# The two writes of the gate rows to DRAM, issued by ScalarE instead of SyncE

## The reference

```
x = x + attention(channel_norm(x))         # 8x8 windows, 4 heads of 16 channels, a bias per head and offset
t = tokens(x)                              # 65536 tokens of 64 channels
p = softmax(norm(t) @ router_w + router_b) # 8 experts
top_p, top_i = top_k(p, 2);  top_p = top_p / sum(top_p)
t = t + sum over the two chosen experts of  top_p * (norm(t) @ expert_w[i] + expert_b[i])
```

## Time and profile before

| what | value |
|---|---|
| median of 3 runs | 1083.46 us |
| the profiled execution | 1089.38 us |
| its span | 1087.6 us |
| PE busy | 1017.8 us, 94% |
| DVE busy | 826.2 us, 76% |
| ACT busy | 797.9 us, 73% |
| POOL busy | 431.8 us, 40% |
| mean granted TensorE clock | 0.988 |

### The profile page before, as it was taken

The page is one execution under the profiler, slowest core; times in us unless marked ns, Lnnn a source line. Parts: engine busy times, 40 slices in busy tenths (PEclk is TensorE's granted clock), DMA queues, the critical chain, the costliest instruction groups (busy, mean ns, idle before and its releaser), DMA issues.

```text
span 1087.6 us, 39027 instructions
## 1 busy us (share of the span) xinstructions
PE 1017.8 (94%) x16762; PEld 577.2 (53%) x16762; DVE 826.2 (76%) x1355; ACT 797.9 (73%) x1280; POOL 431.8 (40%) x509
## 2 busy tenths in 40 slices
PE   4898899999999999999999999999999999999868
PEld 3455555555555545556556555555565555555322
DVE  4456887877787778777877787787887887788873
ACT  1498888778788778878888787877888887677410
POOL 1002434334444443444434433444344335544440
PEclk9999999999999999999999999999999999999988
DMA  6003777877777678777777887777777886766764
GB/s 200 1 16 84 160 160 180 205 184 163 179 183 182 169 188 200 173 176 184 170 183 172 199 204 182 172 177 176 175 184 184 205 196 163 174 146 148 194 157 117
DMA packets 44199, 181.20 MB, mean 167 GB/s; under 512 B 9918, under 2 KB 10174, under 8 KB 27900
## 3 DMA queue, kind: packets, MB, share of 16 engines
q1 hardware_dynamic: 44028, 178.71, 68.8%
HBM read 151.15 MB, written 18.87 MB: 156 GB/s over the span
## 4 chain that ended last, share of the span: by engine, by line
PE 84%; DVE 6%; ACT 5%; issue 3%; DMA 1%; POOL 1%; SPq 0%; DVEq 0%; ACTq 0%
PE bank L713 20%; PE bank L592 12%; PE bank L609 11%; PE bank L626 7%; PE bank L566 5%; PE bank L536 5%; PE bank L633 5%; PE bank L576 4%; PE bank L645 3%; PE bank L654 2%; PE bank L664 2%; PE bank L513 2%; ACT lg L1281 2%; DVE gz L1872 2%; PE bank L527 1%
## 5 line engine op out<-in xcount | busy, mean ns | idle before, releaser
L713 PE MATMUL bank<-gz,wex 64*64 64x512 f32 x2048 | 253.4, 606 | 3.5 <-DVE ob L1921 3.5
L1850 DVE TENSOR_REDUCE mx<-bank 128x16 f32<-128x1024 f32 x128 | 156.2, 1220 | 109.0 <-PE bank L592 108.6
L1659 POOL TENSOR_TENSOR gz<-gz,tt 128x1024 f32<-128x1024 f32 x94 | 226.8, 2427 | 25.6 <-DMA gz<-gates_dram 25.6
L1872 DVE TENSOR_TENSOR gz<-gz,tt 128x1024 f32<-128x1024 f32 x156 | 200.9, 1306 | 1.6 <-DMA gz<-gates_dram 1.5
L1857 DVE TENSOR_TENSOR probs<-bank,mx 128x1024 f32<-128x1024 f32 x128 | 156.7, 1224 | 43.7 <-PE bank L609 40.6
L1620 POOL TENSOR_TENSOR tt<-prj,xs 128x512 f32<-128x512 f32 x64 | 81.7, 1300 | 251.9 <-ACT prj L1270 251.9
L609 PE MATMUL bank<-cst,probs 128*128 128x128 f32 x1024 | 166.6, 285 | 1.8 <-ACT pt L1253 1.3
L1253 ACT ACTIVATE pt<-bank 128x512 f32<-128x512 f32 x256 | 151.0, 590 | 21.9 <-PE bank L609 19.7
L609 PEld LDWEIGHTS bank<-cst,probs 128*128 128x128 f32 x1024 | 108.1, 140 | 97.7 <-issue 60.8
L592 PE MATMUL bank<-km,qs 32*64 32x128 f32 x4096 | 143.7, 276 | 4.6 <-issue 3.1
L592 PEld LDWEIGHTS bank<-km,qs 32*64 32x64 f32 x4096 | 112.2, 133 | 63.4 <-issue 62.8
(11 more groups left out here) (123 smaller groups left out, 1399.0 us busy)
## 6 DMA issues: line engine op xcount, KB each, us to landing
gz<-gates_dram SPq DMA_DIRECT2D x250, 512.0 KB, 7.2
xs<-in_x SPq DMA_DIRECT2D x32, 512.0 KB, 7.4
tt<-tt SPq DMA_DIRECT2D x64, 128.0 KB, 6.6
out<-ob SPq DMA_DIRECT2D x32, 256.0 KB, 6.1
out<-ob SPq DMA_DIRECT2D x64, 128.0 KB, 6.0
gz<-in_rel SPq DMA_DIRECT2D x1, 2048.0 KB, 9.3
gates_dram<-gt_rs SPq DMA_DIRECT2D x64, 32.0 KB, 1.7
cst<-in_consts SPq DMA_DIRECT2D x1, 359.0 KB, 2.8
```

The source lines that it names most:

```text
L713: last = mm(bank[64 * (a ^ x):64 * (a ^ x) + 64, Y_BANK + x, :], wex[64 * a:64 * a + 64, e, :], gz[64 * a:64 * a + 64, s.pair(e)[1], e % 2 ...
L1659: tt_(gz[:, k, e % 2, :], gz[:, k, e % 2, :], tt[s.buf(4)][:, :], op=ALU.mult).then_inc(z_pool, 1)
L1850: red(mx[g % 2][:, :], two_banks(S_BANK).rearrange("p (c k) -> p c k", k=N), axis=AX_X, op=ALU.max).then_inc(max_done, 1)
L1872: tt_(gz[:, k, e % 2, :], gz[:, k, e % 2, :], tt[s.buf(4)][:, :], op=ALU.mult).then_inc(z_dve, 1)
```

## The change

`write_gates` moves from SP's list to ScalarE's, unchanged in itself: the same wait, the same two transfers, the same semaphore. All 32 calls are taken out of SP's list, and in ScalarE's list one stands behind every `move_gates`.

```
@@ SP's stream
-            def write_gates(s):
-
-                sp.wait_ge(gsb_ready, s.count(2, 1))
-                for x in range(2):
-                    sp.dma_start(gates_dram[s.buf(4)][:, x * CH:(x + 1) * CH], gt_rs[s.buf(2)][96 + 16 * x:112 + 16 * x, :]
-                                 ).then_inc(gates_written, 16)
...
             for c in range(8, 31):
-                write_gates(strips[c - 5])
                 spread_gates(strips[c - 5], 0)
                 swap_tokens(strips[c - 6])
...
-            write_gates(strips[-1])
             swap_tokens(strips[-2])
             store(strips[-3])
             spread_gates(strips[-1], 3)
@@ ScalarE's stream
+            def write_gates(s):
+
+                act.wait_ge(gsb_ready, s.count(2, 1))
+                for x in range(2):
+                    act.dma_start(gates_dram[s.buf(4)][:, x * CH:(x + 1) * CH], gt_rs[s.buf(2)][96 + 16 * x:112 + 16 * x, :]
+                                  ).then_inc(gates_written, 16)
...
                 move_scaled_gates(strips[c - 4])
                 move_gates(strips[c - 4])
+                write_gates(strips[c - 4])
                 log_sums(strips[c - 3], 3)
                 exps(strips[c - 2], 1)
```

More of the change, by code:

```diff
@@ L385, in _ @@
             load(strips[4])
-            write_gates(strips[0])
             spread_gates(strips[0], 0)
@@ L391, in _ @@
             spread_gates(strips[0], 3)
-            write_gates(strips[1])
             spread_gates(strips[1], 0)
@@ L398, in _ @@
             spread_gates(strips[1], 3)
-            write_gates(strips[2])
             swap_tokens(strips[1])
@@ L416, in _ @@
                 spread_gates(strips[c - 5], 3)
-            write_gates(strips[-6])
             spread_gates(strips[-6], 0)
@@ L425, in _ @@
             spread_gates(strips[-6], 3)
-            write_gates(strips[-5])
             store(strips[-7])
@@ L433, in _ @@
             spread_gates(strips[-5], 3)
-            write_gates(strips[-4])
             spread_gates(strips[-4], 0)
@@ L438, in _ @@
             spread_gates(strips[-4], 3)
-            write_gates(strips[-3])
             spread_gates(strips[-3], 0)
@@ L447, in _ @@
             spread_gates(strips[-3], 3)
-            write_gates(strips[-2])
             spread_gates(strips[-2], 0)
@@ L1401, in _ @@
             move_gates(strips[0])
+            write_gates(strips[0])
             exps(strips[2], 1)
@@ L1486, in _ @@
             move_gates(strips[-5])
+            write_gates(strips[-5])
             log_sums(strips[-4], 3)
@@ L1522, in _ @@
             move_gates(strips[-4])
+            write_gates(strips[-4])
             seed_bias(strips[-2], 2)
@@ L1557, in _ @@
             move_gates(strips[-3])
+            write_gates(strips[-3])
             seed_bias(strips[-1], 2)
@@ L1585, in _ @@
             move_gates(strips[-2])
+            write_gates(strips[-2])
             move_pt(strips[-1], 6)
@@ L1598, in _ @@
             move_gates(strips[-1])
+            write_gates(strips[-1])
         @block.gpsimd
```

## The result

The changed kernel takes 1093.47 us (median of 5 runs, 1089.18 to 1094.59), the kernel before beside it 1084.01 (1083.02 to 1085.18): a ratio of 1.0076, 95% interval 1.0053 to 1.0098. The changed kernel is slower: later than the predicted 1084.6, and outside of the range, which ended at 1091.5. The slower rival, "ScalarE is held longer than its room" (1091.4), came closest.

A forecast was written before the change was run, and what follows sets the result against it. The prediction saw TensorE with 84% of the chain and SP with 0%; slow pairs 0.5, strip 0 0.3 and strip 30 0.3 added 1.1 us to 1083.46, giving 1084.6, with an 8-in-10 range of 1081.5 to 1091.5.

The forecast's parts named there:

- The slower rival: ScalarE: a late issue or dearer transfer delays the pair beyond its 0.69 us room; 1091.4 us, chance 0.30.
- Taken from SP, 0: SP's queue: 64 issues and 32 waits go, but spreading still waits for the same landing; 0 us.
- When the write starts: ScalarE's sequencer: it reaches the transfer early, so the first write starts beside the second gate move as before; 0 us.
- What the write costs ScalarE in the middle: Strip 13: a pair of 0.79 delays `log_sums` by 0.33 within 0.69 of room; nothing reaches TensorE.
- one of the signs of being wrong, a pair above 1.2: ScalarE's issues: a pair of writes taking above 1.2 us, where about 0.8 was forecast.
- The slow pairs: Strips 7, 8 and 19: pairs of 1.55 to 1.56 exceed the room, 0 to 1.1 us on TensorE's path; 0.5 taken.
- The bound of 1.19: Issue price on ScalarE: SP's longest issue, 1192 ns, taken as upper bound, two making 2.4 us.
- Strip 0, 0.3: First strip: the chain runs over ScalarE without room, so the writes of 0.88 delay `exps` by 0.3 us.
- strip 30, 0.3: Last strip but one: the probabilities' move comes 0.33 late, some 0.05 is taken up; 0.3 us.
- Strip 31, 0: Last strip: ScalarE has no work behind the writes, SP's swap and store go out earlier; 0 either way.
- the 2.4 us piece among DVE's gate steps: End of kernel: L1890 takes 2.43 beside POOL's product; its absence would show the forecast wrong on the faster side.

The follow-up runs named there:

- The four strips 0, 1, 2 and 30: Against the kernel before, only the writes of strips 0, 1, 2 and 30 moved to ScalarE, the other 28 pairs on SP: 1088.56 us, ratio 1.0040.
- the short hold: Kernel before, writes on SP, plus an unused 256-column ACTIVATE on ScalarE behind every pair of gate moves: 1086.46 us, ratio 1.0024.
- the shift: Changed kernel with 80 bias-row products done twice, putting TensorE's later instructions 160 places back: 1089.96 us, ratio 1.0045 to the kernel before.
- last-five: Against the kernel before, only the writes of strips 27 to 31 moved to ScalarE, the others on SP: 1087.02 us, ratio 1.0022.
- full-turn: Changed kernel with 128 bias-row products done twice, 256 more TensorE instructions at the start: 1095.98 us (one run).
- the middle trace: Against the kernel before, only the writes of strips 3 to 26 moved to ScalarE, the others on SP: 1086.81 us, ratio 1.0028.
- the long added instruction: Kernel before, writes on SP, plus an unused 1280-column ACTIVATE on ScalarE behind the gate moves of eleven strips: 1093.81 us, ratio 1.0087.
- the late version: Changed kernel with both writes later on ScalarE, behind the probabilities' move and before the values' move: 1087.51 us, ratio 1.0039 to the kernel before.
- the single transfer: Changed kernel with the two writes made one transfer of 32 rows at the same place on ScalarE: 1091.17 us, ratio 1.0061 to the kernel before.
- the first three strips alone: Against the kernel before, only the writes of strips 0, 1 and 2 moved to ScalarE, the others on SP: 1083.27 us, ratio 1.0002.
- the rest's: Against the kernel before, the writes of all strips but 0, 1, 2 and 30 moved to ScalarE, those four on SP: 1087.03 us, ratio 1.0019.

## Why the prediction was wrong

The step that failed is the price of the pair where ScalarE's list is on the chain without room: it was taken as that of an undisturbed pair, added once, in strips 0 and 30 alone, 0.6 us in all. The four strips 0, 1, 2 and 30 measured 4.3 us (1.2 to 7.5).

*Taken from SP, 0: right.* SP waits for the landing as before, and no wait of the products for spread rows has grown.

*When the write starts: right.* 500.77 is the end of the first move plus 0.03, beside the second one. The first half of the slower rival (a late start) is refuted; its second half, a pair dearer on ScalarE than its room, is what came, though in some strips and not in most. The rule of the Trainium skill ("Perfetto Trace Analysis", "DMA Instruction — HWDGE"), that the sequencer stays occupied until the descriptors are made, agrees with the trace, and the prediction drew too little from it: in strip 6 ScalarE stands 1.26 while its second write takes 1.41.

*What the write costs ScalarE in the middle: right for the pair as such.* 0.78 against the forecast 0.79, delay 0.38 against 0.33, idle before the values' move 0.45 against "towards 0.5", and no wait of TensorE in strip 13. One write per strip on ScalarE costs 1.0010, the short hold in all strips 1.0024, both not told from none. But one of the signs of being wrong, a pair above 1.2, is there in ten strips.

*The slow pairs, "0 to 1.1; I take half, 0.5": the wrong reading of the rows.* The long second writes of the earlier trace rows were taken for a matter of strips 7, 8 and 19, and perhaps of SP's full queue. They belong to neither: they go with the fetching of TensorE's instructions, and the shift shows that they move with it. So other strips can have one too; ten to fifteen second writes are above 0.5 us in each trace with both writes on one engine, and they take up to 1.84. The bound of 1.19, the worst of one trace on SP, was no bound: with the short added instruction SP's own second write in strip 2 took 1.77. I had the rows for it: 64 issues whose long ones had no cause that I could name, one of them in strip 2 (1.17), which I did not price. Whether the term was too small isn't settled: the 28 strips other than 0, 1, 2 and 30 measured 1.0019, 2.1 us against 0.5, with an interval from -1.0 to 5.2.

*Strip 0, 0.3, and strip 30, 0.3: the terms that failed.* The places were right: ScalarE's list is on the chain there and has no room. But each was priced by the undisturbed pair, added once, and strips 1 and 2 were not looked at. The four strips measured 1.0040, 4.3 us (1.2 to 7.5), against 0.6; the traces of the changed kernel show 3.2 to 4.0 from strip 0 to 3 and 2.5 to 2.7 from 30 to 31.

Two things make the difference. The pairs are held in these strips too (1.45, 2.17 and 1.39 in strips 0, 2 and 30). And the delay grows behind ScalarE: in strip 30 from 1.00 at the probabilities' move to 2.7 at the logits of the last strip, 0.72 of it where TensorE ran at 1.2 GHz and 0.97 in POOL's residual. I treated waits as of fixed length; they were not.

The slow clock alone isn't the loss of strip 30: in the last-five and the full-turn trace the move is 1.01 and 0.78 late, the transposes run at 2.4 GHz, and the stretch still takes 31.39 and 31.16; in the middle trace the clock is low without a hold, and it takes 30.07. Over all sixteen traces the stretch is 31.2 to 32.1 in the eight where ScalarE issues the whole of strip 30's rows in front of the probabilities' move, in two transfers or one, or has the long added instruction there, and 28.8 to 30.2 in the eight others.

That holding ScalarE is enough for a loss of this size, and that the rows' way isn't needed for it, is shown by the added ACTIVATE of 1.26 us (1.0087, with no transfer moved). What decides the clock in strip 30 is shown in part only: the transposes there ran at 1.2 GHz in six of the nine traces with ScalarE held in front of them, and in one of the seven without; the short hold of 0.3 left it at 2.4. By these counts a hold makes the slow clock likelier and does not fix it.

*Strip 31, 0: not contradicted.* The last stretch lies between 43.6 and 48.5 us over the traces of all kernels, whoever issues the writes, and the 2.4 us piece among DVE's gate steps is there in the changed kernel as well, at another step: L1890 takes 2.43 in the trace of before alone, and after it is L1981 that takes 2.33, at 1054.47. The swap and the store did go out earlier, at 1043.65 and 1051.41 in place of 1059.77 and 1060.95.

Open are how the loss is shared between the four strips and the loop, the half of the late version's loss (1.0039), the loss of the single transfer (1.0061), the 1.0002 of the first three strips alone beside a trace with 4 us more, and what held the second write in strip 30. No version beat the kernel before.

## What to carry to other kernels

Here a transfer issued by ScalarE held its list for as long as the issue took, less what the engine still had to do, and where there was no room the long issues set the price, not the median: 1.19 us in the trace of before and up to 1.84 in the one after, against 0.4. The longest issue of a single trace is no bound. Before moving an issue, look for places where the new engine's list is on the chain without room (here the first strips and the last but one), price these by the longest issue and ask what TensorE's clock does in the added wait. Two transfers in a row on a computing engine were the dear case here; dividing them between two engines saved the loss, and merging them into one did not.

## What the runs showed of the hardware that was not expected

- A second transfer issued right behind a first on the same engine takes 0.42 to 0.44 us undisturbed, and mostly 0.5 to 1.84 while a 16 KB packet of TensorE's instructions (queue q8) is in flight. It was seen on SP and on ScalarE. Not every packet holds one: in strip 18 of the kernel before the write took 0.42 with a packet starting 0.1 into it. And besides strip 30 five shorter holds, of 0.54 to 0.74, had no q8 packet beside them (strip 14 before and in the last-five trace, 24 in the middle one, 3 and 24 in the rest's); in four of these a packet of 8 KB of another instruction queue, q14, was in flight. A first one of 16 rows takes 0.31 to 0.37, and of two on two engines at the same time the one 0.32 and the other 0.36.
- These packets come at fixed places of TensorE's stream, one for some 252 instructions, so 160 more instructions at the start moved the held strips, and 256 more put most of them back.
- A single transfer of 32 rows is issued in 0.58 to 0.60, less than two of 16 rows (0.75), and was held once in 32.
- ScalarE's sequencer runs ahead of the engine by about two instructions: in the late version a pair of 0.78 starting at 437.74 in strip 11, while an ACTIVATE of 1.05 from 437.59 ran, left no gap on ScalarE.
